# A new order of one pair of heads in the cross-attention: the next pair's queries and first keys ahead of this pair's last product, both low halves on GpSimd, and the values one step earlier

## The reference

```python
q = (layernorm(x) @ w_q)     # x: 2 x 256 x 256, 16 heads of 64
k = (ctx_1024 @ w_k)         # ctx_1024: 2 x 4096 x 256
v = (ctx_1024 @ w_v)
scores = einsum('bhqd,bhkd->bhqk', q, k) * 64 ** -0.5
out = einsum('bhqk,bhkd->bhqd', softmax(scores), v)
x = x + out.reshape(2, 256, 1024) @ w_o
```

## Time and profile before

| | |
|---|---|
| median of 3 runs | 1440.27 us (1438.49 to 1441.47) |
| the profiled execution's own time | 1439.66 us |
| span of its trace | 1437.9 us |
| PE busy | 1300.4 us, 90% |
| DVE busy | 977.8 us, 68% |
| ACT busy | 870.2 us, 61% |
| POOL busy | 243.4 us, 17% |

### The profile page before, as it was taken

The page is one execution under the profiler, slowest core; times in us unless marked ns, Lnnn a source line. Parts: engine busy times, 40 slices in busy tenths (PEclk is TensorE's granted clock), DMA queues, the critical chain, the costliest instruction groups (busy, mean ns, idle before and its releaser), DMA issues. The chain is left out here.

```text
span 1437.9 us, 22817 instructions
## 1 busy us (share of the span) xinstructions
PE 1300.4 (90%) x8447; PEld 1004.9 (70%) x8447; DVE 977.8 (68%) x1249; ACT 870.2 (61%) x1543; POOL 243.4 (17%) x245
## 2 busy tenths in 40 slices
PE   4999999999999999899999999999999969898763
PEld 3887777877777868687778787778686844567522
DVE  4658586767677777665767676777767646557366
ACT  4757575858575766575858585757666612444242
POOL 4203020202121121020202021211212111120000
PEclk9999999999999999999999999999999979998876
DMA  4000000000000001300000000000000043534000
GB/s 164 1 2 19 1 20 2 19 1 19 15 6 16 1 19 31 88 19 1 20 1 19 2 20 14 6 21 1 16 1 5 1 152 72 60 45 52 1 0 15
DMA packets 29684, 34.70 MB, mean 24 GB/s; under 512 B 3985, under 2 KB 26001, under 8 KB 29329
## 3 DMA queue, kind: packets, MB, share of 16 engines
q1 hardware_dynamic: 27536, 29.83, 7.9%
q0 software_dynamic: 2048, 3.43, 1.6%
HBM read 25.89 MB, written 0.52 MB: 18 GB/s over the span
## 5 line engine op out<-in xcount | busy, mean ns | idle before, releaser
L463 DVE TENSOR_TENSOR prob_sum<-prob_sum,probs 128x1024 f32<-128x1024 f32 x224 | 264.5, 1223 | 164.6 <-ACT probs L382 163.9
L382 ACT ACTIVATE probs<-scores_a 128x1024 f32<-128x1024 f32 x128 | 131.1, 1025 | 209.2 <-PE scores_a L578 208.1
L315 POOL TENSOR_TENSOR k_split<-prob_sum,k_split 64x512 fp32r<-64x512 f32 x128 | 164.7, 1287 | 303.9 <-ACT prob_sum L358 303.9
L442 DVE TENSOR_REDUCE step_max<-scores_a 128x2 f32<-128x1024 f32 x128 | 156.8, 1225 | 37.3 <-PE scores_a L566 35.4
L442 DVE TENSOR_REDUCE step_max<-scores_b 128x2 f32<-128x1024 f32 x128 | 155.7, 1216 | 0.0
L577 PE MATMUL scores_a<-q_twice,k_split 128*128 128x256 f32 x512 | 139.2, 305 | 5.0 <-ACT q_low_max L373 4.9
L308 POOL TENSOR_TENSOR w_lo<-w_raw,w_hi 128x768 fp32r<-128x768 f32 x16 | 34.9, 2181 | 593.8 <-ACT w_hi L327 593.8
L382 ACT ACTIVATE probs<-scores_b 128x1024 f32<-128x1024 f32 x128 | 131.3, 1026 | 0.0
L577 PE MATMUL scores_b<-q_twice,k_split 128*128 128x256 f32 x512 | 128.4, 283 | 0.0
L578 PE MATMUL scores_a<-q_low_max,k_ones 128*128 128x256 f32 x512 | 128.0, 283 | 0.0
L578 PE MATMUL scores_b<-q_low_max,k_ones 128*128 128x256 f32 x512 | 128.0, 283 | 0.0
(11 more groups left out here) (213 smaller groups left out, 2627.4 us busy)
## 6 DMA issues: line engine op xcount, KB each, us to landing
ctx_rows<-in_ctx_dram SPq DMA_DIRECT2D x10, 512.0 KB, 3.6
w_raw<-in_L_xattn_w_v_dram SPq DMA_DIRECT2D x14, 256.0 KB, 3.2
probs<-in_ctx_dram SPq DMA_DIRECT2D x6, 512.0 KB, 6.1
grouped<-dots_sb SPq DMA_DIRECT2D x16, 136.0 KB
grouped<-dots_sb POOLq DMA_DIRECT2D x16, 136.0 KB, 13.1
w_raw<-in_L_xattn_w_q_dram SPq DMA_DIRECT2D x16, 128.0 KB, 2.4
w_raw<-in_L_xattn_w_k_dram SPq DMA_DIRECT2D x16, 128.0 KB, 2.5
wo_pair<-in_L_xattn_w_o_dram SPq DMA_DIRECT2D x16, 128.0 KB, 2.1
```

The source lines that it names most:

```text
L315: pool.tensor_tensor(k_split[0:DH, B, keys], k_staged_b[j % 2], k_split[DH:P, B, keys].bitcast(F32), ALU.subtract).then_inc(k_low[B], 1)
L382: act.activation(probs[:, j % 2, h, :], flat_scores[h], ACT.Exp, scale=SCALE).then_inc(exp_done, 1)
L442: dve.tensor_reduce(step_max[:, :, 1 - h, j - 1], scores[h][:, :, :], X, ALU.max).then_inc(max_done, 1)
L463: dve.tensor_tensor(prob_sum[:, h, :], prob_sum[:, h, :], probs[:, j % 2, h, :], ALU.add).then_inc(sum_done, 1)
```

## The change

- PE: the next pair's `project_q` and `project_k(0)` stand ahead of `product_with_v(7)` of this pair (not across a batch's end). `sum_over_keys` of the pair before stands behind k1 (behind k0 in a batch's first pair) and `project_output` behind s1. Values begin at j = 3, behind s1, so that only v6 stands between s7 and the transposes.
- The low halves of both heads are made by POOL from one staged copy of all 128 rows, which lies in `probs` now; DVE's line 435 is gone. One semaphore `k_low` counts both.
- `v_bank` is swapped: v0 goes into `v_ps` and waits for `q_low`, v1 goes into `out_ps` and waits for `y_added`.
- ACT: `split_weights` of the next pair stands behind the exponentials of chunk 3, the high queries and the first high keys behind those of chunk 7; copies of the values come one step earlier.
- DVE: `divide` stands ahead of the maxima of chunk 0 at j = 1, and `add_output` behind `low_queries`, ahead of the maxima of the third chunk.
- The loop runs two turns in each batch instead of three, and three pairs are unrolled behind it instead of one.

```diff
...
@@ -215,11 +215,12 @@
             body(b * PAIRS, b, 0, 0)
-            with eng.Fori(0, PAIRS // 2 - 1) as k:
+            with eng.Fori(0, PAIRS // 2 - 2) as k:
                 for parity in (1, 0):
                     i = k * 2 + (2 - parity)
                     body(b * PAIRS + i, b, i, parity)
-            body((b + 1) * PAIRS - 1, b, PAIRS - 1, 1)
+            for i in range(PAIRS - 3, PAIRS):
+                body(b * PAIRS + i, b, i, i % 2)
         def context_banks(n):
@@ -312,9 +316,12 @@
                     keys = slice(j * CHUNK, (j + 1) * CHUNK)
                     pool.wait_ge(k_staged, STEPS * it + j + 1)
                     pool.wait_ge(k_high, 2 * (STEPS * it + j) + 2)
-                    pool.tensor_tensor(k_split[0:DH, B, keys], k_staged_b[j % 2], k_split[DH:P, B, keys].bitcast(F32),
-                                       ALU.subtract).then_inc(k_low[B], 1)
-                pool.wait_ge(k_low[B], STEPS * (it + 1))
+                    staged = k_staged_rows[j % 2]
+                    pool.tensor_tensor(k_split[DH:P, A, keys], staged[0:DH], k_split[0:DH, A, keys].bitcast(F32),
+                                       ALU.subtract).then_inc(k_low, 1)
+                    pool.tensor_tensor(k_split[0:DH, B, keys], staged[DH:P], k_split[DH:P, B, keys].bitcast(F32),
+                                       ALU.subtract).then_inc(k_low, 1)
+                pool.wait_ge(k_low, 2 * STEPS * (it + 1))
             pool.wait_ge(consts_ready, 5)
             for b in range(BATCH):
                 pairs_of_batch(pool, b, body)
@@ -337,25 +344,39 @@
                     own = v_near[:, tiles, :] if half == parity else v_far[:, half, tiles, :]
                     act.activation(own, src[:, :, 0:PAIR], ACT.Copy).then_inc(v_copied, 1)
-            def body(it, b, i, parity):
-                if not is_first(it):
-                    split_weights(it, b, i)
-
+            def high_queries(it):
                 act.wait_ge(q_made, it + 1)
                 for h in (A, B):
                     for half in (0, DH):
                         act.activation(q_twice[half:half + DH, h, :], v_ps[h * DH:(h + 1) * DH, 0:SEQ],
                                        ACT.Copy).then_inc(q_high, 1)
+
+            def high_keys(it, j):
+                keys = slice(j * CHUNK, (j + 1) * CHUNK)
+                act.wait_ge(k_made, STEPS * it + j + 1)
+                ps = k_ps[j % 2]
+                act.activation(k_split[0:DH, A, keys], ps[0:DH, :], ACT.Copy).then_inc(k_high, 1)
+                act.activation(k_split[DH:P, B, keys], ps[DH:P, :], ACT.Copy).then_inc(k_high, 1)
+
+            def stage_keys(it, j):
+                if j >= 2:
+                    act.wait_ge(k_low, 2 * (STEPS * it + j - 1))
+                elif not is_first(it):
+                    act.wait_ge(sum_done, 2 * STEPS * it - 2)
+                    act.wait_ge(pv_done, STEPS * it - 1)
+                act.activation(k_staged_rows[j % 2], k_ps[j % 2][:, :], ACT.Copy).then_inc(k_staged, 1)
+
+            def body(it, b, i, parity):
+                if is_first(i):
+                    if b > 0:
+                        split_weights(it, b, i)
+                    high_queries(it)
                 for j in range(STEPS + 1):
                     if j < STEPS:
                         keys = slice(j * CHUNK, (j + 1) * CHUNK)
-                        act.wait_ge(k_made, STEPS * it + j + 1)
-                        ps = k_ps[j % 2]
-                        act.activation(k_split[0:DH, A, keys], ps[0:DH, :], ACT.Copy).then_inc(k_high, 1)
-                        act.activation(k_split[DH:P, B, keys], ps[DH:P, :], ACT.Copy).then_inc(k_high, 1)
-                        if j >= 2:
-                            act.wait_ge(k_low[B], STEPS * it + j - 1)
-                        act.activation(k_staged_b[j % 2], ps[DH:P, :], ACT.Copy).then_inc(k_staged, 1)
+                        if j > 0 or is_first(i):
+                            high_keys(it, j)
+                        stage_keys(it, j)
                     if j > 0:
                         keys = slice((j - 1) * CHUNK, j * CHUNK)
@@ -364,9 +385,8 @@
                                        ).then_inc(k_copied, 1)
                         act.activation(k_ones[DH:P, B, keys], k_split[DH:P, B, keys].bitcast(F32), ACT.Copy
                                        ).then_inc(k_copied, 1)
-                    if j > 3:
-                        copy_v(b, i, parity, j - 4)
-                copy_v(b, i, parity, STEPS - 3)
+                    if j > 2:
+                        copy_v(b, i, parity, j - 3)
                 copy_v(b, i, parity, STEPS - 2)
                 act.wait_ge(maxT_made, it + 1)
@@ -375,6 +395,8 @@
                     for h in (A, B):
                         n = 2 * (STEPS * it + j) + h
                         act.wait_ge(scores_made, n + 1)
+                        if j == 0 and h == A:
+                            act.wait_ge(k_low, 2 * STEPS * (it + 1))
                         if j >= 2 or not is_first(it):
                             act.wait_ge(sum_done, n - 3)
@@ -383,8 +405,13 @@
                                        ).then_inc(exp_done, 1)
                     if j == 0:
                         copy_v(b, i, parity, STEPS - 1)
+                    if j == 3 and stays_in_batch(i):
+                        split_weights(it + 1, b, i + 1)
                     if next_group(b, i, j) is not None:
                         context_high(act, next_group(b, i, j))
+                if stays_in_batch(i):
+                    high_queries(it + 1)
+                    high_keys(it + 1, 0)
                 if next_group(b, i, STEPS) is not None:
                     context_high(act, next_group(b, i, STEPS))
             for b in range(BATCH):
@@ -424,18 +451,9 @@
                                       ALU.subtract).then_inc(q_low, 1)
                     dve.tensor_tensor(q_low_max[DH:P, B, :], v_ps[DH:P, 0:SEQ], q_twice[DH:P, B, :].bitcast(F32),
                                       ALU.subtract).then_inc(q_low, 1)
-                if not is_first(it):
-                    divide(it - 1)
                 for j in range(STEPS + 1):
-                    if j < STEPS:
-                        keys = slice(j * CHUNK, (j + 1) * CHUNK)
-                        n = STEPS * it + j
-                        ps = k_ps[j % 2]
-                        dve.wait_ge(k_high, 2 * n + 1)
-                        dve.tensor_tensor(k_split[DH:P, A, keys], ps[0:DH, :], k_split[0:DH, A, keys].bitcast(F32),
-                                          ALU.subtract).then_inc(k_low[A], 1)
                     if j == 1 and not is_first(it):
-                        add_output(it - 1, last_batch(b, i))
+                        divide(it - 1)
                     if j > 0:
                         for h in (A, B):
                             dve.wait_ge(pre_made, 2 * (STEPS * it + j - 1) + h + 1)
@@ -443,6 +461,8 @@
                                               ).then_inc(max_done, 1)
                     if j == 2:
                         low_queries()
+                    if j == 2 and not is_first(it):
+                        add_output(it - 1, last_batch(b, i))
                 dve.wait_ge(max_done, 2 * STEPS * (it + 1))
                 dve.tensor_reduce(row_max[:, :, :], step_max[:, :, :, :], X, ALU.max).then_inc(max_chain, 1)
                 dve.wait_ge(max_chain, 2 * it + 1)
@@ -541,9 +561,9 @@
                     todo = todo[len(todo) // 2:] if tiles else todo[:len(todo) // 2]
                 for (m, half, for_next), t in todo:
                     if t == 0 and m == 0:
+                        pe.wait_ge(q_low, 2 * it + 2)
+                    elif t == 0 and m == 1:
                         wait_past(pe, y_added, it)
-                    elif t == 0 and m == 1:
-                        pe.wait_ge(q_low, 2 * it + 2)
                     elif t == 0:
                         pe.wait_ge(v_copied, v_before(b, i) + m - 1)
                     width = 2 * PAIR if for_next else PAIR
@@ -557,7 +577,7 @@
             def scores_for_max(it, j):
                 keys = slice(j * CHUNK, (j + 1) * CHUNK)
                 for h in (A, B):
-                    pe.wait_ge(k_low[h], STEPS * it + j + 1)
+                    pe.wait_ge(k_low, 2 * (STEPS * it + j) + h + 1)
                     if j > 0:
                         pe.wait_ge(max_done, 2 * (STEPS * it + j - 1) + h + 1)
                     else:
@@ -608,32 +628,34 @@
                 last.then_inc(y_made, 1)
             def body(it, b, i, parity):
-                project_q(it, b)
-                if not is_first(it):
-                    sum_over_keys(it - 1)
-                pe.wait_ge(w_low, it + 1)
+                if is_first(i):
+                    project_q(it, b)
                 for j in range(STEPS):
                     if j >= 2:
-                        pe.wait_ge(k_low[A], STEPS * it + j - 1)
```

(23 more changed lines are left out.)

8 lines of the change are left out of this document (5 added, 3 removed).

## The result

The changed kernel takes 1445.45 us in the median of 10 runs, the kernel before 1439.64 in 10 runs beside it: 1.0044 times as long, with a 95% interval of 1.0029 to 1.0059. The forecast was no change, 1438.6 us. The profiled executions have spans of 1443.6 and 1437.9 us, 5.7 us apart.

A forecast was written before the change was run, and what follows sets the result against it. PE was taken to set the pace, busy 66.17 of 69.03 us a pair. Gains of 8.4 us less costs of 3.4, 2.1 and 1.5 gave 1438.3, adjusted to 1438.6 us, no change; range 1432.5 to 1446.5.

The forecast's parts named there:

- The wait for the fold: Between pairs, PE's idle time of 1.59 us for DVE's folded sums before line 598 would be gone.
- in front of v0 for the low queries: v0 overwrites the queries in `v_ps`, so PE would wait for DVE's low queries: 1.8 us lost.
- in front of the transposes for `neg_max`: With only v6 between s7 and the transposes, PE would wait 1.1 us there, where it had not waited.
- The taken branches: Loop branch on PE between last product and k1, one taken per batch: 2 x 1.7 = +3.4 us.
- pair 8: A batch's first pair, without early q: low queries done at about 617.2 plus 2.3, costing +1.5 us.
- the sum: Whole kernel: -8.4 (14 pairs at 0.6) + 3.4 + 2.1 + 1.5 = -1.4 us against 1439.66.
- The walk: Following the queues through one pair by row durations: a period of 68.3 us, 0.7 less than 69.03.
- third rival: Stops at v0 and the transposes cost 0.5 us a pair beyond their waits: slower, 1445.3 us; chance 0.20.
- pair 0: A batch's first pair: v0 starts where it did, but k4 and s2 are still to come, +2.1 us.
- fourth rival: PE's clock falls behind the 1.8 us in front of v0, 2.2 us in 14 pairs: +31, 1469; chance 0.05.
- The 1.59 us: PE's idle time before line 598 in the kernel before, which brought no fall of the clock; used against that rival.
- a gain of nothing: Upper end of the forecast range, pairs gaining nothing: 1446.5 us.

The follow-up runs named there:

- the second experiment: The changed kernel with VectorE's two low queries put ahead of the division instead of behind the maxima of s1: 1417.63 us, 0.9841 of the kernel before.
- the late-values kernel: The changed kernel with its values begun a step later, v0 behind s2, as in the kernel before: 1409.19 us, 0.979 of the kernel before.

## Why the prediction was wrong

*Right, by its own steps.* The wait for the fold goes. PE stops in front of v0 for the low queries (1.8 us forecast, 1.66 found) and in front of the transposes for `neg_max` (1.1 and 1.17), and loses 0.46 at s1 (0.55). Phase two is reached 38.0 us behind q (37.8). The taken branches cost 3.6 us (3.4), pair 8 costs 1.9 (1.5). GpSimd is hardly late in this order (0.4 us in all at line 586's B halves), and the long fold of the earlier trace rows is 1.2 us in all 16 pairs. VectorE's maxima still take 1.22 us each beside both low halves on GpSimd. The low queries bind v0, as the second experiment shows.

*The step that failed is the sum,* in the term "I take 0.6 us a pair ... 14 pairs ... -8.4". Measured were 4.8 us, 0.34 a pair. The walk's 68.3 us was 0.2 short of the written-out pairs (68.49) and 0.35 short of the loop's (68.66), and the four pairs beside a batch's ends, which I counted like the others, gained 0.03 to 0.25. That is 3.6 us of the 9.6 between the forecast's -1.4 and the account's +8.2. It is the largest share but does not decide the sign by itself: my own third rival named 0.29 us as the point from which it decides, and 0.34 came, which with the costs as forecast is +2.2. Another 3.0 are the clock, 1.4 the context's transfers and 1.0 pair 0, and the rest pair 8 and the branches. It landed on slower, but not by the third rival's price: the stops cost what the walk gave them.

*What carried it over to slower was the fourth rival at another place and another size,* a term that the sum put at nothing. I had the clock fall in front of v0 in 14 pairs for 31 us or not at all. It fell in the batches' last pairs, where the values are 128 wide, behind either stop, twice in each of the two traces, for 1.5 us each. The 1.59 us that I used against it lie between wide matmuls, and for such places the argument held (1.39 us did nothing in any mid-batch pair). A bound from a row at another kind of work was no bound for the last pairs. Leaving the stops out in these two pairs gave 7.8 us: 2.8 to 2.9 a pair for the stops and 1.5 for the clock were expected to give 8.7.

*Smaller:* pair 0 cost some 3 instead of 2.1 us. From v0 on it takes 2.4 us more than before, near the 2.33 that k4 and s2 take; v0 itself came 7.66 and 7.16 us behind the first scores in the two traces, against 7.24 before, and the first scores come 0.3 and 0.6 us later, for which no cause was looked for. The context's transfers in pair 7 (1.4 us) were not in the sum at all; why they come later against PE was not tried. The upper end of the range, "a gain of nothing", is 1447.0 by the forecast's own terms, not 1446.5, and the lower end 1433.0. That the measured 1445.45 lies inside the range is luck: the upper end stood for no gain at all, and the pairs did gain, while costs came that the sum didn't have. I corrected for half of the 0.6 us between one execution and the median; the start alone varies by 2.6 us.

*The branch.* The sum by the rule of the Trainium skill ("Advanced Engine Details and Errata", Control Flow Timing, about 108 ns) would have been 3.2 us lower. The runs contradict it for taken branches: 1.6 to 2.2 us of idle PE each, and about 7 us of the late-values kernel for two of them with the clock behind them and the loop's other pairs.

*And the larger point.* The prediction took the new order as one thing with a small net. It is three, in the order in which they were put together here: early queries (-0.33%, some -5 us, alone), the low half on GpSimd (-1.8%, -25 us, behind them) and early values (+2.5%, +37 us, on both). It had the 2.9 us a pair of stops that the early values make in its own walk, and did not ask what the order would be worth without them.

## What to carry to other kernels

When a wait goes, walk on to the next producer and ask at once whether the step that meets it there could stand elsewhere: here one step later for the values, or VectorE's low queries in its idle time before the division, was worth 28 to 36 us where the change as a whole lost 6. A net gain of tenths per iteration can't be forecast by its sign from a walk with tenths of error; say so in the chances. Look at iterations of another shape one by one, since a stop of 1.0 us in front of the transposes cost its 1.2 us in the pairs with wide work, and in the two with narrow work mostly 1.5 us more. And take a second trace of each kernel before booking 2 or 3 us of one on a cause.
